# Late expert rows: 22 whole tiles and 5 shared ones instead of 30 whole tiles

## The reference, cut to what matters

```python
scores = softmax(h @ gate_w.T)                  # 2048 rows, 8 experts
topk_w, topk_ids = _grouped_topk(scores)        # 2 experts a row, weights sum to 1
# for each picked expert e of a row h (256 values):
#   gate, up = split(h @ w13[e].T)              # 2 x 512 values
#   y = (silu(gate) * up) @ w2[e].T             # 256 values
# out = sum of topk_w * y over the two experts
```

## Time and profile before

| | |
|---|---|
| median of 3 runs | 552.25 us (551.52 to 552.89) |
| the profiled execution | span 551.1 us from first to last instruction; no other time of it is given |
| PE busy | 538.4 us, 98% of the span |
| granted TensorE clock | 0.999 of full speed over the span |
| POOL busy | 168.7 us, 31% |
| additions of a tile, L422 | 39, of 1.57 us on POOL each |
| DMA | 74.30 MB |

### The profile page before, as it was taken

One profiled execution on the slowest core, in us unless ns is written; L12 is line 12 of the kernel. 1 busy time (PEld: TensorE's weight loads), 2 busy tenths in 40 slices (PEclk: granted clock), 3 DMA queues, 4 the chain that ended last, 5 costly groups with the idle time before them and its releaser, 6 DMA issues.

```text
span 551.1 us, 11061 instructions
## 1 busy us (share of the span) xinstructions
PE 538.4 (98%) x3967; PEld 444.4 (81%) x3968; DVE 284.0 (52%) x847; ACT 254.1 (46%) x587; POOL 168.7 (31%) x152
## 2 busy tenths in 40 slices
PE   9999999999999999999999889999999999999995
PEld 7887878777655676777777679999999999999995
DVE  4867676988562776855788865722212111212110
ACT  1343476263346767687787834542222222222221
POOL 2211000002145222332222043354335454445533
PEclk9999999999999999999999999999999999999999
DMA  8940000000110000300470657968788888898733
GB/s 320 403 141 1 2 0 2 0 1 2 38 39 0 2 2 1 116 1 2 135 287 7 227 172 244 318 187 268 221 246 219 248 229 236 239 255 238 239 66 38
DMA packets 28651, 74.30 MB, mean 135 GB/s; under 512 B 5600, under 2 KB 20320, under 8 KB 23360
## 3 DMA queue, kind: packets, MB, share of 16 engines
q1 hardware_dynamic: 18592, 61.87, 31.9%
q0 software_dynamic: 7488, 10.39, 10.6%
q10 hardware_dynamic: 2528, 1.48, 0.9%
HBM read 62.88 MB, written 10.85 MB: 134 GB/s over the span
## 4 chain that ended last, share of the span: by engine, by line
PE 93%; ACT 4%; DVE 1%; issue 1%; POOL 0%; DVEq 0%; POOLq 0%
PE ps L897 64%; PE ps L1193 12%; PE ps L901 11%; ACT ring L617 2%; PE ps L1041 1%; PE ps L1050 1%; ACT ring L624 1%; PE ps L1053 1%; PE ps L1044 1%; PE ps L981 1%; PE ps L1024 1%; ACT HF L629 0%; ACT ring L658 0%; POOL out_x L422 0%; PE ps L1122 0%
## 5 line engine op out<-in xcount | busy, mean ns | idle before, releaser
L897 PE MATMUL ps<-keep,arena 128*128 128x128 f32 (+2 forms) x976 | 114.9, 274 | 0.0
L897 PEld LDWEIGHTS ps<-keep,arena 128*128 128x128 f32 x976 | 112.8, 192 | 1.5 <-issue 1.1
L2014 DVE TENSOR_TENSOR keep<-keep,ps 128x512 f32<-128x512 f32 x39 | 26.8, 686 | 145.7 <-PE ps L897 124.2
L422 POOL DMA_INDIRECT out_x<-arena,row_no x38 | 59.9, 1576 | 102.1 <-DMA out_x<-arena,row_no 65.2
L1193 PE MATMUL ps<-arena,keep 128*128 x312 | 73.7, 380 | 0.1
L665 ACT COPY keep<-ps 128x256 f32<-128x256 f32 x39 | 14.5, 372 | 107.1 <-PE ps L901 103.8
L381 POOL TENSOR_TENSOR ring<-arena,keep 128x512 f32<-128x512 f32 x32 | 33.5, 1049 | 96.9 <-PE ps L897 79.8
L1193 PEld LDWEIGHTS ps<-arena,keep 128*128 128x128 f32 x312 | 56.4, 190 | 6.6 <-issue 0.3
L617 ACT ACTIVATE ring<-ps,mx 128x128 f32<-128x128 f32 x192 | 52.3, 403 | 6.2 <-DVE mx L1714 6.2
L897 PE MATMUL ps<-ring,arena 128*32 128x128 f32 (+1 forms) x640 | 53.1, 348 | 1.5 <-ACT ring L624 1.4
L373 POOL TENSOR_TENSOR var_x<-var_x,minus_half 128x4 f32<-128x4 f32 x16 | 16.5, 1036 | 115.8 <-DVE var_x L1570 115.8
(11 more groups left out here) (266 smaller groups left out, 816.2 us busy)
## 6 DMA issues: line engine op xcount, KB each, us to landing
arena<-in_w SPq DMA_DIRECT2D x29, 1024.0 KB
w_first<-in_w SPq DMA_DIRECT2D x10, 1024.0 KB
arena<-in_w SPq DMA_DIRECT2D x8, 512.0 KB, 7.3
keep<-in_keep SPq DMA_DIRECT2D x1, 3115.0 KB, 20.8
ring<-in_fold SPq DMA_DIRECT2D x1, 2112.0 KB, 12.7
arena<-in_x SPq DMA_DIRECT2D x4, 512.0 KB, 10.5
arena<-in_ctxT SPq DMA_DIRECT2D x4, 512.0 KB, 7.1
arena<-in_ctx SPq DMA_DIRECT2D x4, 384.0 KB, 11.2
```

The lines of the kernel that those rows point to most:

```text
L422: pool.indirect_dma_start(out=out_d, out_offset=bass.IndirectOffsetOnAxis(ap=rows_at, axis=0), in_=YO[t % DEEP], in_offset=None, compute_o ...
L897: ins = pe.matmul(out, w, m, start=(k == 0), stop=(k == len(pairs) - 1))
L2014: dve.tensor_tensor(HA[r % 2], HA[r % 2], ps[:, 2 * (r % 2) + 1, :], ALU.mult).then_inc(act_ok, 1)
```

## The change

The 2944 picks that the nine early tiles leave are laid out differently. Each expert gets whole tiles as before, but an expert's remainder of up to 64 rows no longer opens a whole tile: 22 late tiles are whole, and five are shared, with two strips of 64 rows, each of an expert of its own. So there are 9 + 22 + 5 = 36 tiles. The shared ones stand at tiles 15, 19, 23, 27 and 31.

In a shared tile the rows are the stationary operand, 64 at a time, and the weights are streamed, in two column strips of the array. The result then has rows on partitions, so the product of silu and up is transposed on PE (`turn_act`) and copied back by ACT (`act_turned`) before down. The two experts' `w13` go to two buffers of their own, and ACT copies their `w2` to two more. Its addition is made in two of 64 rows, the second after the first has landed. All tiles are written out, without a loop. The late routing on DVE gets a new part, `late_halves`, and longer `late_tiles`, `late_hot` and `late_rows`.

```diff
+HALF = P // 2
+LEFT = B * S * NPICK - EARLY * P
+HALVES = LEFT // HALF + NE - 1
+LATE = HALVES // 2 - NE // 2
+SHARED = -(-HALVES // 2) - LATE
+WHOLE, STRIPS, PLACES = EARLY + LATE, 2 * SHARED, LATE + 2 * SHARED
+NT = WHOLE + SHARED
+SPLIT_AT = tuple(NT - 5 - 4 * n for n in reversed(range(SHARED)))
...
+            def weights_of_halves(n):
+                if n:
+                    sp.wait_ge(u_ps, SPLIT_AT[n - 1] + 1)
...
+                for h in range(2):
+                    weights(WHOLE + 2 * n + h, W13_HALF[h], half_in)
...
+                if c >= DEEP:
+                    sp.wait_ge(u_ps, ran[c - DEEP] + 1)
+                weights(c, W13[c % DEEP], w13_in[c % DEEP])
+                if t + 1 in SPLIT_AT[1:]:
+                    weights_of_halves(SPLIT_AT.index(t + 1))
+                if c == EARLY + 1:
+                    weights_of_halves(0)
...
+                if t in SPLIT_AT:
+                    for n in range(2):
+                        own = slice(HALF * n, HALF * (n + 1))
+                        rows_at = row_upper[:, c - WHOLE:c - WHOLE + 1] if n else row_no[0:HALF, c:c + 1]
+                        if n:
+                            pool.wait_ge(added, 16 * (adds_up_to(t) - 1))
+                        pool.indirect_dma_start(out=out_d, out_offset=bass.IndirectOffsetOnAxis(ap=rows_at, axis=0),
+                                                in_=YO[t % DEEP][own, :], in_offset=None, compute_op=ALU.add).then_inc(added, 16)
+                    return
...
+            def w2_of_halves(n):
...
+                for h in range(2):
+                    c = WHOLE + 2 * n + h
+                    e = act.value_load(e_id[0:1, c:c + 1], min_val=0, max_val=NE - 1)
+                    act.copy(W2_HALF[h], w2e[:, bass.ds(e * W2_N, W2_N)]).then_inc(w2_half, 1)
+
+            def act_turned(r):
+                act.wait_ge(at_ps, split_up_to(r))
+                act.copy(HA[r % 2], bank(FEED)).then_inc(at_ok, 1)
...
+            def gate_up_halves(r):
...
+                for g in range(2):
+                    for k in range(KD):
+                        for h in range(2):
+                            own = slice(HALF * h, HALF * (h + 1))
+                            at = (2 * k + g) * INTER
+                            ins = pe.matmul(ps[own, 2 * (r % 2) + g, :], XIT[r % 2][:, k, own], W13_HALF[h][:, at:at + INTER], start=(k == 0), stop=(k == KD - 1))
+                    ins.then_inc((g_ps, u_ps)[g], 1)
+
+            def turn_act(r):
+                pe.wait_ge(act_ok, r + 1)
...
+                for i in range(INTER // P):
+                    ins = turn(bank(FEED)[:, i * P:(i + 1) * P], HA[r % 2][:, i * P:(i + 1) * P])
+                ins.then_inc(at_ps, 1)
+
+            def down_halves(r):
+                pe.wait_ge(at_ok, split_up_to(r))
+                pe.wait_ge(w2_half, 2 * split_up_to(r))
+                pe.wait_ge(y_ok, r - 1)
+                for i in range(INTER // P):
+                    for h in range(2):
+                        own = slice(HALF * h, HALF * (h + 1))
+                        ins = pe.matmul(Y_PS[r % 2][own, :], HA[r % 2][:, i * P + HALF * h:i * P + HALF * (h + 1)], W2_HALF[h][:, i * D:(i + 1) * D],
+                                        start=(i == 0), stop=(i == INTER // P - 1))
+                ins.then_inc(y_ps, 1)
+
+            def step(r):
+                turn_in(r + 2)
+                if r in SPLIT_AT:
+                    turn_act(r)
+                if r + 1 in SPLIT_AT:
+                    gate_up_halves(r + 1)
+                else:
+                    gate_up(r + 1)
+                if r in SPLIT_AT:
+                    down_halves(r)
+                else:
+                    down(r)
...
+            def late_halves():
...
+                dve.tensor_scalar(bases[:, 0, :], l_rest, float(P), None, ALU.mult)
+                dve.scalar_tensor_tensor(l_rest, l_rest, -float(P), n_left, ALU.mult, ALU.add)
+                settle()
...
+                dve.tensor_tensor(c8s, l_rest.unsqueeze(2).broadcast_to([P, NE, STRIPS]), kept("half_start").unsqueeze(1).broadcast_to([P, NE, STRIPS]), ALU.is_gt)
+                settle()
+                dve.tensor_reduce(h_n, c8s, AXX, ALU.add)
+                settle()
...
             def late_tiles():
...
+                dve.tensor_tensor(cmp2.rearrange("p (v n e) -> p v n e", v=4, e=NE), every.unsqueeze(1).broadcast_to([P, 4, PICKS, NE]),
+                                  bases[:, :, :].unsqueeze(2).broadcast_to([P, 4, PICKS, NE]), ALU.mult)
...
+                dve.tensor_reduce(base_of[:, :], cmp2.rearrange("p (n e) -> p n e", e=NE), AXX, ALU.add)
...
             pick(4)
             pick(5)
+            late_halves()
             late_tiles()
             late_hot()
             gated(5)
```

More of the change, by code:

```diff
@@ L85, in build @@
         spare_yo = arena[:, 2 * LANE + 2048:2 * LANE + 3072]
+        W13_HALF = [arena[:, 3 * LANE + n * W13_N:3 * LANE + (n + 1) * W13_N] for n in range(2)]
         keep = sb("keep", [P, KEEP_N])
@@ L157, in build @@
         PQ = [split(ring[:, 1024 * n:1024 * n + 1024], HT8) for n in range(4, 6)]
+        W2_HALF = [ring[:, 1024 * n:1024 * n + W2_N] for n in range(4, 6)]
         by_query = sb("by_query", [P, 2 * D])
@@ L214, in build @@
         e_min = spare[15][:, 0:NT]
+        ends = sb("ends", [P, 7, NE])
+        l_full, l_off, l_end, l_rest, h_n, h_off, h_end = (ends[:, n, :] for n in range(7))
+        bases = sb("bases", [P, 4, NE])
+        base_of = sb("base_of", [P, 4 * PICKS])
+        full_rows, full_at, half_at, odd_at = (base_of[:, n * PICKS:(n + 1) * PICKS] for n in range(4))
+        col_all = picks_at[:, 2:4, :].rearrange("p f n -> p (f n)")
+        beyond, upper, in_half = (sb(t, [P, PICKS]) for t in ("beyond", "upper", "in_half"))
+        odd_i = sb("odd_i", [P, NE], mybir.dt.int32)
+        e_half = sb("e_half", [P, STRIPS])
+        swapped = sb("swapped", [P, 2, SHARED])
         scratch = arena[:, NG * LANE + 1536:NG * LANE + 2048]
@@ L268, in build, with split_up_to, column, adds_up_to @@
         XT_PS, Y_PS = ps[:, 4, 0:D], [ps[:, 5 + u, 0:D] for u in range(2)]
[L270 to L279, removed]
+        assert SPLIT_AT[0] > EARLY + 2
+        def split_up_to(r):
+            return sum(t <= r for t in SPLIT_AT)
+        def column(r):
+            return WHOLE + split_up_to(r) - 1 if r in SPLIT_AT else r - split_up_to(r)
+        def adds_up_to(r):
+            return r + 1 + split_up_to(r)
         def bank(k):
@@ L685, in _ @@
+            def act_turned(r):
+                act.wait_ge(at_ps, split_up_to(r))
+                act.copy(HA[r % 2], bank(FEED)).then_inc(at_ok, 1)
+            def step(r):
+                turned(r + 2)
+                answer(r - 1)
+                if r in SPLIT_AT:
+                    act_turned(r)
+                gate(r + 1)
+                if r + 3 in SPLIT_AT:
+                    w2_of_halves(SPLIT_AT.index(r + 3))
+            act.wait_ge(set_ok, 2)
             for n in range(2):
@@ L1515, in _ @@
             turn_x4_half(3, 1)
[L1516 removed]
+            gate_up(2, (0,))
             gate_logits(3)
[L1518 to L1531 removed]
@@ new lines, in _ @@
+            down(3)
+            down(4)
+            gate_up(5, (0,))
+            gate_up(5, (1,))
+            gate_up(6, (0,))
+            place_late()
+            turn_in(7)
+            down(5)
+            gate_up(6, (1,))
+            gate_up(7, (0,))
+            turn_in(8)
+            down(6)
+            gate_up(7, (1,))
+            gate_up(8, (0,))
+            gate_up(8, (1,))
+            turn_in(9)
+            down(7)
+            gate_up(9, (0,))
+            gate_up(9, (1,))
@@ L1557, in _ @@
+            turn_in(10)
+            down(8)
+            turn_pair()
+            for r in range(EARLY, NT - 2):
+                step(r)
+            gate_up(NT - 1)
+            down(NT - 2)
+            down(NT - 1)
             same_sums()
```

420 lines of the change are left out of this document (228 added, 192 removed).

## The result

The changed kernel takes 574.4 us (569.6 to 580.5, four runs) where the kernel before takes 552.3 beside it. That is 1.037 times the kernel before, interval 1.0325 to 1.0419. Forecast was 551.8, with a range of 543 to 559. The profiled execution took 572.47 us, its span is 570.7 (before: 551.1).

A forecast was written before the change was run, and what follows sets the result against it. The prediction took POOL's serial additions as the bound: tile 5's start 3.7 us later, 61.9 to tile 15, then 81.7 and 29.2, put tile 34's at 544.4, -0.4 us against tile 37's before; so 551.8 us, range 543 to 559.

The forecast's parts named there:

- The bound: End of the kernel: POOL's serial additions into out_x decide, with PE's answers ready some 11 us early.
- the price of a whole addition among weights: Tiles 15 to 27 on POOL: nine whole additions at 5.65 us each, against 5.37 before.
- 61.9 us as now: POOL, from tile 5's addition to tile 15's: the same 61.9 us as in the kernel before.
- The eight halves of tiles 15 to 27: Shared tiles' 64-row additions on POOL in the mixed stretch: eight at 3.85 us each.
- Tile 5's start: Tile 5's addition on POOL, at 367.88 before, moves by 3.7 to 4.8 us; 3.7 taken.
- The half: A 64-row addition on POOL: issue at the low end, 0.79 us; 3.2 alone, 3.85 in the mixed stretch.
- nearly a whole: Rival: a half addition costs 4.6 us mixed, 4.0 alone; kernel at 558 us (555 to 562); chance 0.21.
- The stall at place_late: PE waits 3.7 us (2.5 to 4.8) at place_late for DVE's longer late routing.
- Strips overlap: Shared tiles on PE: strips overlap fully, each tile costing 0.54 us more: 0.44 for transposes, 0.1 for two strip passages.
- PE's own end: PE's end moves by -16.56 + 2.7 + 3.7 = -10.2 us: tiles removed, shared tiles, stall.
- additions keep up: Rival: halves at 3.2 us and whole additions at 5.2; kernel at 542.5 us (541 to 547); chance 0.25.
- Rows late: Fetches queued behind late additions on POOL make PE wait for gathered rows, at no further cost.

The follow-up runs named there:

- e4_no_chain: Changed kernel with each tile's rows stored to a place of its own by plain DMA instead of added to the output; 543.2 us, 0.983 of the kernel before.
- b_burst: Kernel before, with weight loads of three tiles (13, 14, 15 and so on) issued together and the fourth alone; 570.3 us, 1.031.
- b_halves: Kernel before, with six whole additions (tiles 11, 15, 19, 23, 27, 31) each made as two of 64 rows; 573.9 us, 1.0388.
- e10_neither: e7_early_id without each shared tile's second load and second addition; 545.3 us, 0.9873 of the kernel before.
- e7_early_id: Changed kernel, each load from tile 13 waiting for an addition's issue mark, the expert's number read before that wait; 551.1 us, 0.9984 of the kernel before.
- f_best: e7_early_id with PE's place_late one product and down product later, DVE's gating of tiles 5 and 6 before the late tables; 550.7 us, 0.995.

## Why the prediction was wrong

*The bound* was named rightly: the additions, not PE (e4_no_chain). *The step that failed is the price of a whole addition among weights*, "5.65 for a whole one (5.37 now, one load in four more)". The nine of tiles 16 to 26 took 64.7 us, 7.2 each: 13.9 us more than forecast, of the 20.2 by which tile 34's start missed. The burst was seen, but its cost was taken as a share of time with weights in flight. It is set, for nine tenths of the loss, by where a load falls: in the kernel before, loads and additions both come about once in 5.5 us, and from tile 15 to 31 each load is issued 2.1 to 4.6 us after an addition's start, never in its issue. So 5.37 was the price of that step, not of an addition among weights. Both changes of the rhythm that were tried in that kernel, by loads (b_burst) and by halves (b_halves), lose it; in the changed kernel a load fell 0.1 us before the start of tile 16's addition and another 1.4 us behind it.

*The other terms.* From tile 5's addition to tile 15's, "61.9 us as now": 64.7, mainly as tile 6's met five loads issued between 373 and 382 us and took 9.9 (379.4 to 389.3; before 6.3), and tile 13's met the first burst and took 9.2 (before 6.0), while others got shorter. The eight halves of tiles 15 to 27: 32.8 us for 30.8 predicted; whole stretch 15 to 27 with both, 97.5 for 81.7. Tiles 28 to 33: 30.0 for 29.2. Tile 5's start: 372.3, 0.7 later than the sum took (the forecast's own text on the routing had 372.7). Together 0.7 + 2.8 + 15.8 + 0.8 = 20.1.

*The half.* The low end of the issue, 0.79, was wrong: 1.43, against 1.58 for a whole one, so the issue hardly goes with the rows. Alone a half is 3.6 and not 3.2, mixed 4.1 and not 3.85, which by itself would have made 554 to 555; the rival "nearly a whole" (4.0 alone, 4.6 mixed, deciding from 4.1 on) was reached at its lower border only, and the halves' own price explains 3 us of the miss and not 22. The Trainium skill, "DMA: Bandwidth & Descriptors", "Anatomy of one DMA — SWDGE (gpsimd) path", by which half the bytes would save an estimated 0.15 us, does not fit: 4.57 became 3.36 and 3.82. Nor does its estimate for a whole addition, 2.15 us, reach the 3.0 that the rows show beyond the issue, though the forecast said that the two agree.

*PE.* The stall at place_late was right (3.5 for 3.7). Not seen was the clock behind it, which costs 2.4 us; PE comes to place_late 0.7 earlier than before, so tile 5's answer ends 5.3 us later. Strips overlap, but a shared tile costs 23.0 - 4 x 5.52 = 0.95 us and not 0.54; less the four transposes, 0.44, that leaves 0.5 for its two strip passages, where the forecast took 0.1. So PE's own end moves by -16.56 + 4.8 + 5.3 = -6.5 and not -10.2. That is near what the runs have: PE's last product ends 6.9 us earlier in e4_no_chain and 7.5 in e10_neither, which is 7.1 faster. The rival "additions keep up" has its size from that: 545 rather than 542.5.

*Rows late* came true (16.8 us), with no share in the end, as PE was not the bound; e4_no_chain has none. The 2% that the chain of waits puts down to them stand before the additions of tiles 22 and 26, whose answers had been ready for 12 to 14 us.

What delays an addition beside a load was seen only as packets that start late and take longer. The Trainium skill, "DMA: Bandwidth & Descriptors", "Queues, rings and completion order", says that each DMA engine turns from queue to queue and drains a whole packet before it switches. The traces agree as far as they go: a load alone moves for some 3.5 us, and no addition's first row came later than 3.8 us after the end of its issue, though up to three loads were queued. That the engines wait for this reason is not shown.

## What to carry to other kernels

A serial chain of small DMAs beside big loads had no fixed price here: read where each load is issued against each link, and treat a mean taken from a steady rhythm as a property of the rhythm. Where the rhythm is to change, tie the loads to the links (here a mark behind each addition) before judging the change. Price a split link from a run: two halves of an addition cost 2.6 us more than one whole of 4.57, with nothing beside them.

## What was not expected of the hardware

A load issued 0.5 us after a half's start made it 7.75 us; issued 1.7 to 1.9 us after an addition's start it left 3.4 to 6.1 (e7_early_id, tiles 15 to 30). After a 3.5 us stall PE was granted a mean clock of 0.57, so that most of these 6.8 us ran at the lower level, 1.2 GHz, and then 1.00 again; f_best, without that stall, was granted 1.00 there. After the first of two halves the next addition starts 0.6 us after the last row has moved, after a whole one 1.1 us.
